# A graph network's attention stage: the pick matrices get 128 rows, and the products that use them read all rows of the turned codes

## The chip, the cores and the metric

The kernel runs on one core of a Trainium2 chip. The metric is the device time of one execution in microseconds (us); lower is better. The core has a matrix engine (TensorE, PE in the profile, with its weight loads as PEld), a vector engine (VectorE, DVE), an activation engine (ScalarE, ACT), GpSimd (POOL), which here issues the indirect transfers, and SyncE (SP), which issues the plain ones. They run on their own and wait for each other through semaphores.

## What is computed

The input is a graph of 6,250 nodes with 64 features and 206,250 edges, sorted by destination. A message network comes first and then two attention layers:

```python
h = relu(layernorm(x))
x = x + L0(h, ...)          # edge MLP, segment sum over row, node MLP
h = relu(layernorm(x))
# attention layer: heads=4, ch=32, then heads=1, ch=64
h = (x @ W).reshape(n, heads, ch)
alpha_src = sum(h * a_src, -1); alpha_dst = sum(h * a_dst, -1)
e = alpha_src[src] + alpha_dst[dst]
e = where(e > 0, e, 0.2 * e)
m = segment_max(e, dst); ex = exp(e - m[dst])
alpha = ex / (segment_sum(ex, dst)[dst] + 1e-16)
out = segment_sum(h[src] * alpha, dst) + b
```

The result is x plus the output of the second layer.

## The kernel before

Nodes lie in 49 tiles of 128. Edges are worked on in groups of 512 (four chunks u of 128), and all edges of a group have their destination in one tile of nodes. There are 452 groups (`GROUPS`) in each attention layer; `LAYERS` gives four heads with 32 channels and then one head with 64.

Every engine runs its own `attend` in a loop over the groups, unrolled by eight (`SLOTS`), and each works on several groups at different stages at once; `of(k)` is the group that entered k steps ago. The order within a step is that of the code, and nothing else. For one group the stages are:

- SP loads the ids of the 512 edges (L521). POOL gathers the table rows of the sources, with four indirect transfers (L690). It waits until the messages of the group eight before are made (`msg_ready`) and its codes are turned.
- DVE turns the lane number of each edge's destination into a code of 16 numbers (`edge_codes`, L1461 to L1477): 0 where a bit agrees and -BIG where it doesn't. ACT makes a matrix of ones and zeros, which says to which lane an edge belongs (`a_hot`, L829 and L836).
- PE transposes that matrix (L1072) and the codes together with the shares of the source (L1076). ACT copies both out of PSUM into `turned` (L853, of which only the first 28 or 19 rows are written, and L855).
- PE multiplies with the pick matrices (L1117), once for each head: the result shows, for each lane and each of 512 edges, the share of the source, or about -BIG where the edge is not the lane's. DVE takes the maximum (`largest_shares`, L1490 for pairs of heads, L1486 for one head), and from it makes the new shift of each node (`new_shifts`, L1516 to L1538).
- PE looks up shares and shifts for each edge (L1088). DVE makes the logits (L1556 to L1567), ACT the exponential (L843), DVE the messages (L1576). ACT makes an f32 copy of `a_hot` (L861).
- PE sums the messages by lane (L1100, f32), and DVE adds them to the node's sum (L1588, L1593).

In a step PE does L1072 and L1076, then L1088, L1100 and last L1117, each for another group. Of the pick products' operands the matrix `picks[n]` has 16 + 3 x heads rows: 28 in layer 0 and 19 in layer 1. It is filled once: cleared on POOL, with ones set by L560, and the first 16 rows copied by DVE. `turned` has 128 rows, eight slots, two halves and 512 columns in bf16; half 0 is the transposed `a_hot`, half 1 the codes.

Ahead of each layer DVE makes the table of node rows (L1422 to L1445) and raises `table_ready`; SP then writes the table to memory (L504), and the gathers start behind that.

Of the kernel before, what the change touches and what calls it, by code (L numbers as in the profile page):

```python
# [13 lines left out]
BF16 = mybir.dt.bfloat16  # L14
# [5 lines left out]
P = 128  # L20
# [27 lines left out]
CODE = 16  # L48
CODE_WORDS = CODE // 2
SLOTS = 8  # L50
# [5 lines left out]
LAYERS = ((HEADS, CH), (1, OUT_DIM))  # L56
# [118 lines left out]
def gnn_kernel(nc, x, ids_in, src_in, dst_next, rec_in, ew1, eb1, ew2, eb2, nw1, nb1, nw2, nb2,  # L175
               W1, a_src1, a_dst1, b1, W2, a_src2, a_dst2, b2, out):
    ctx = ExitStack()
    with ctx:
        def sb(name, shape, dt=F32):
            return ctx.enter_context(nc.sbuf_tensor(name, shape, dt))[tuple(slice(None) for _ in shape)]  # L180

        def sem(name):
            return ctx.enter_context(nc.semaphore(name))
# [32 lines left out]
        spare = sb("spare", [P, SLOTS * U])  # L216
        signs_at = sb("signs_at", [P, NB + 1])

        picks = [sb(f"pick{n}", [CODE + 3 * h, h, P], BF16) for n, (h, _) in enumerate(LAYERS)]
        lower = sb("lower", [P, P])  # L220
        ones = sb("ones", [P, P])
        ones_b = sb("ones_b", [P, P], BF16)
# [53 lines left out]
        def carve(start, shape, dt=F32):  # L276
            words = 1
            for n in shape:
                words *= n
            words = words if dt != BF16 else words // 2  # L280
            v = arena[:, start:start + words]
            assert start + words <= ARENA, (start, shape)
            if dt != F32:
                v = v.bitcast(dt)
            names = " ".join("abcd"[:len(shape)])
            kw = {"abcd"[n]: shape[n] for n in range(len(shape))}
            return v.rearrange(f"p ({names}) -> p {names}", **kw), start + words
# [62 lines left out]
        turned, at = carve(at, [SLOTS, 2, GE], BF16)  # L350
# [21 lines left out]
        def S(name):  # L372
            if name not in s:
                s[name] = sem(name)
            return s[name]
# [3 lines left out]
        class Rounds:  # L379
# [5 lines left out]
            def load(self, i):  # L385
                _, self.values = nc.values_load_multi_w_load_instructions(
                    self.table[0:1, bass.ds(i - self.back, self.count)], engines=(self.engine,), min_val=0, max_val=self.top,
                    skip_runtime_bounds_check_because="counts of comparisons, and starts that a minimum bounds")

            def of(self, g):  # L390
                if g.i is None:
                    return self.eng.value_load(self.table[0:1, bass.ds(g.at, 1)], min_val=0, max_val=self.top)
                return self.values[g.off + self.back]
# [472 lines left out]
        def _(pe):  # L866
# [9 lines left out]
            for k in range(2):  # L876
                pe.matmul(ps[7][:, 128 * k:128 * k + NB], lower, counts[k], start=True, stop=True)
                pe.matmul(ps[7][:, 128 * k + 64:128 * k + 64 + NB], ones, counts[k], start=True, stop=True)
                mm = pe.matmul(ps[7][0:NB, 256 + k:257 + k], counts[k], ones[:, 0:1], start=True, stop=True)
# [3 lines left out]
            for b in range(len(BATCHES) + 1):  # L883
                if b < len(BATCHES):
                    if b > 1:
                        pe.wait_ge(S("own_tt"), b - 1)
                    for u, t in enumerate(BATCHES[b]):
                        mm = pe.transpose(ps[b % 2][0:F_IN, u * P:(u + 1) * P], hs[:, t, :], ident)
                    mm.then_inc(S("own_t"), 1)
                if b > 0:  # L890
# [3 lines left out]
                    for u, t in enumerate(BATCHES[b - 1]):  # L894
                        pe.matmul(ps[2 + (b - 1) % 2][:, u * F_HID:(u + 1) * F_HID], tile_t[0:F_IN, (b - 1) % 2, 0, u * P:(u + 1) * P],
                                  w_dst, start=True, stop=True)
                        mm = pe.matmul(ps[4][:, u * F_HID:(u + 1) * F_HID], tile_t[0:F_IN, (b - 1) % 2, 0, u * P:(u + 1) * P],
                                       w_src, start=True, stop=True)
# [9 lines left out]
            for k in range(3):  # L908
                mm = pe.matmul(ps[4 + k][:, 0:lone], gap_wide[0][0:NT - 1, :], reached[0:NT - 1, k * lone:(k + 1) * lone],
                               start=True, stop=True)  # L910
# [96 lines left out]
            for b in range(len(BATCHES) + 2):  # L1007
                if b < len(BATCHES):
# [4 lines left out]
                    for u, t in enumerate(BATCHES[b]):  # L1013
                        mm = pe.transpose(ps[2 + b % 2][:, u * P:(u + 1) * P], agg[:, t, :], ident)
                    mm.then_inc(S("node_t"), 1)
                if 0 < b <= len(BATCHES):
                    c = b - 1
                    n = len(BATCHES[c]) * P
# [5 lines left out]
                if b > 1:  # L1024
# [4 lines left out]
                    for u, t in enumerate(BATCHES[c]):  # L1029
                        mm = pe.matmul(ps[6 + c % 2][:, u * F_IN:(u + 1) * F_IN], mid_t[:, c % 2, u * P:(u + 1) * P], w_out,  # L1030
                                       start=True, stop=True)
                    mm.then_inc(S("node_out"), 1)

            for n, (heads, ch) in enumerate(LAYERS):
# [5 lines left out]
                for b in range(len(BATCHES) + 1):  # L1040
                    if b < len(BATCHES):
                        if b > 1:
                            pe.wait_ge(S("gat_tt"), before + b - 1)
                        for u, t in enumerate(BATCHES[b]):
                            mm = pe.transpose(ps[b % 2][0:k_in, u * P:(u + 1) * P], node_in[:, t, :], ident)
                        mm.then_inc(S("gat_t"), 1)
                    if b > 0:
# [4 lines left out]
                        for u, t in enumerate(BATCHES[c]):  # L1052
                            mm = pe.matmul(ps[2 + c % 2][:, u * width:(u + 1) * width], tile_t[0:k_in, c % 2, 0, u * P:(u + 1) * P],
                                           gat_w[n], start=True, stop=True)
# [6 lines left out]
                def attend(of):  # L1061


                    g = of(1)
                    if g is not None:
                        r = g.slot(SLOTS)
                        bank = ps[(4, 7)[g.slot(2)]].bitcast(BF16)
                        if g.back(2).exists():
                            pe.wait_ge(S("turned_copied"), g.back(2).done(2))
                        pe.wait_ge(S("a_hot_ready"), g.done())  # L1070
                        for u in range(U):
                            pe.transpose(bank[:, u * P:(u + 1) * P], a_hot[:, r, u, :], ident_b)  # L1072
                        pe.wait_ge(S("code_ready"), g.done(2))
                        pe.wait_ge(S(f"gathered_{r}"), g.uses(SLOTS, 16 * U))
                        for u in range(U):
                            mm = pe.transpose(bank[:, GE + u * P:GE + (u + 1) * P],  # L1076
                                              g_rows[:, r, u * step:u * step + P // 2].bitcast(BF16), ident_b)
                        mm.then_inc(S("turned"), 1)

                    g = of(5)  # L1080
                    if g is not None:
                        pe.wait_ge(S("max_step"), g.done(MAX_STEPS))
                        if g.back(1).exists():
                            pe.wait_ge(S("logit_step"), g.back(1).done(LOGIT_STEPS))
                        lk = look[:, g.slot(4), 0:6 * heads].rearrange("p (k w) -> p k w", k=3)
                        for u in range(U):
                            for part in range(3):
                                mm = pe.matmul(ps[5][:, u * 2 * heads:(u + 1) * 2 * heads], turned[:, g.slot(SLOTS), 0, u * P:(u + 1) * P],  # L1088
                                               lk[:, part, :], start=(part == 0), stop=(part == 2))
                        mm.then_inc(S("looked_up"), 1)  # L1090

                    g = of(7)
                    if g is not None:
                        out_w = width + heads
                        pe.wait_ge(S("a_hot_f_ready"), g.done())
                        pe.wait_ge(S("msg_ready"), g.done())
                        if g.back(1).exists():
                            pe.wait_ge(S("a_added"), g.back(1).done())
                        for u in range(U):
                            mm = pe.matmul(ps[6][:, 0:out_w], a_hot_f[:, g.slot(4), u, :], g_msg[:, g.slot(4), u * out_w:(u + 1) * out_w],  # L1100
                                           start=(u == 0), stop=(u == U - 1))
                        mm.then_inc(S("a_summed"), 1)

                    g = of(2)
                    if g is not None:
                        pe.wait_ge(S("turned_copied"), g.done(2))
                        for h in range(heads):
                            if heads > 1:  # L1110

                                if h % 2 == 0 and g.back(1).exists():
                                    pe.wait_ge(S(f"max_taken{h // 2}"), g.back(1).done())
                            elif g.back(2).exists():
                                pe.wait_ge(S("max_taken0"), g.back(2).done())
                            bank = ps[h] if heads > 1 else ps[g.slot(2)]
                            mm = pe.matmul(bank, picks[n][:, h, :], turned[0:CODE + 3 * heads, g.slot(SLOTS), 1, :], start=True, stop=True)  # L1117
                            if h % 2 == 1 or heads == 1:
                                mm.then_inc(S(f"shown{h // 2}"), 1)

                attention_pipeline(pe, 7, attend, n)

        @block.vector
        def _(dve):
            link = Chain(dve, S("dve_step"))
# [278 lines left out]
            for n, (heads, ch) in enumerate(LAYERS):  # L1404
# [38 lines left out]
                for h in range(heads):  # L1443
                    link(dve.tensor_copy(ac[:, :, h, 0:ch], tb[:, :, at_f + h * ch:at_f + (h + 1) * ch]))
                link(dve.memset(ac[:, :, :, ch:ch + 1], 1.0))  # L1445
                dve.sem_inc(S("table_ready"), 1)

                step = CODE_WORDS + row
# [210 lines left out]
```

## Time and profile before

| | |
|---|---|
| time, median of 3 runs | 9172.81 us (9167.3 to 9173.32) |
| the profiled execution | 9175.25 us, its span 9173.7 us |
| busy: PE | 77% of the span |
| busy: DVE | 66% |
| busy: POOL | 69% |
| busy: ACT | 53% |
| mean granted clock of PE | 0.703 |

The profile page gives the busy time of each engine and, in 40 slices of the span, its share in tenths together with the clock that the chip granted to PE. One slice is 229 us. The edge stage ends at about 4,100 us, layer 0 of the attention runs from 4,320 to 6,745 us and layer 1 from 6,825 to 9,153 us. Other views read the same execution: groups of instructions by line, who waited for whom, the busy time of chosen stretches, the instructions in order of time, and the chain of work that ended last. Instructions of one engine overlap by some tens of nanoseconds, so spacing from start to start is shorter than the durations.

### The profile page before, as it was taken

The numbers are of one execution on the slowest core, as the hardware profiler recorded it, in microseconds if no ns is written. First come the engines' busy times: TensorE is split into PE (matmuls) and PEld (weight loads), VectorE is DVE, ScalarE is ACT, GpSimd is POOL, SyncE is SP. The second block draws the span as 40 slices with busy tenths as digits, with TensorE's granted clock in tenths as the row PEclk, the third lists the DMA queues.
The fourth block names the chain that finished last, engine by engine and source line by source line (L and its number), as shares of the span: only waits on it lengthen the run. The fifth ranks groups of instructions, "written<-read, shape, count | busy, mean of one in ns | idle before, by whom it ended". The sixth has DMA issues, their size and how long they took to land.

```text
span 9173.7 us, 232222 instructions
## 1 busy us (share of the span) xinstructions
PE 7037.3 (77%) x51014; PEld 5502.8 (60%) x51015; DVE 6077.1 (66%) x27239; ACT 4887.5 (53%) x11854; POOL 6338.1 (69%) x7563
## 2 busy tenths in 40 slices
PE   2466666666679999995999999999957777777776
PEld 2355555555568888883566666666635555555554
DVE  7777742222234444444999999999967776676766
ACT  4122233333335455552676767767637777777775
POOL 0377777777777777771777777777737777777775
PEclk9988888888889999996555555555555555555555
DMA  4222222222222222221222222222341111111114
GB/s 141 46 55 55 55 59 60 59 60 60 59 77 80 81 81 80 80 79 25 55 55 54 55 54 54 54 54 55 53 27 28 28 28 28 28 28 28 28 28 27
DMA packets 990523, 491.42 MB, mean 54 GB/s; under 512 B 830665, under 2 KB 841468, under 8 KB 990140
## 3 DMA queue, kind: packets, MB, share of 16 engines
q0 software_dynamic: 168832, 302.29, 15.1%
q1 hardware_dynamic: 701756, 169.41, 10.0%
q10 hardware_dynamic: 119840, 18.68, 1.2%
q8 instruction: 31, 0.51, 0.0%
q14 instruction: 64, 0.52, 0.0%
HBM read 356.46 MB, written 151.48 MB: 55 GB/s over the span
## 4 chain that ended last, share of the span: by engine, by line
PE 24%; issue 24%; POOL 24%; DVE 17%; DMA 6%; DVEq 2%; ACT 1%; POOLq 1%; SPq 0%; ACTq 0%
POOL z_s L640 18%; POOL arena L690 6%; DMA arena<-table,arena 5%; PE ps_all L965 5%; PE ps_all L975 4%; PE ps_all L1100 3%; PE ps_all L992 3%; PE ps_all L989 2%; DVE shift L1531 2%; DVE arena L1535 2%; DVE arena L1490 2%; PE ps_all L1076 1%; DVE arena L1576 1%; PE ps_all L1001 1%; PE ps_all L977 1%
## 5 line engine op out<-in xcount | busy, mean ns | idle before, releaser
L690 POOL DMA_INDIRECT arena<-table,arena x3616 | 3479.3, 962 | 1497.8 <-issue 983.5
L640 POOL DMA_INDIRECT z_s<-arena x1660 | 1758.1, 1059 | 852.4 <-issue 504.2
L1100 PE MATMUL ps_all<-arena 128*128 128x132 f32 (+1 forms) x7232 | 1805.1, 428 | 1.8 <-DVE acc L1593 1.8
L1100 PEld LDWEIGHTS ps_all<-arena 128*128 128x128 f32 x7232 | 1603.0, 324 | 2.6 <-issue 2.6
L829 ACT ACTIVATE arena<-lanes_b,arena 128x128 bf16<-128x128 bf16 x3616 | 1147.3, 387 | 416.7 <-DVE arena L1464 388.5
L1490 DVE TENSOR_REDUCE arena<-ps_all 128x2 f32<-128x1024 f32 x904 | 1096.8, 1213 | 18.3 <-PE ps_all L1117 18.3
L1117 PE MATMUL ps_all<-arena,pick 28*128 28x512 bf16 (+1 forms) x2260 | 1072.1, 591 | 1.8 <-DVE arena L1490 1.8
L1076 PE MATMUL ps_all<-ident_b,arena 128*128 128x128 bf16 x3616 | 537.6, 301 | 651.1 <-DMA arena<-table,arena 445.9
L745 ACT ACTIVATE arena<-ps_all 18x512 f32<-18x512 f32 x415 | 243.6, 587 | 1379.9 <-PE ps_all L952 1376.4
L853 ACT ACTIVATE arena<-ps_all 28x512 bf16<-28x512 bf16 (+1 forms) x904 | 523.4, 579 | 720.1 <-PE ps_all L1076 720.1
L1386 DVE TENSOR_TENSOR arena<-lanes,arena 128x512 f32<-128x512 f32 x452 | 325.4, 720 | 758.4 <-PE ps_all L965 758.4
L950 PE MATMUL ps_all<-ident_b,arena 128*128 128x128 bf16 x1660 | 189.3, 246 | 829.0 <-DVE arena L1334 827.3
L1076 PEld LDWEIGHTS ps_all<-ident_b,arena 128*128 128x128 bf16 x3616 | 353.1, 135 | 768.6 <-DVE arena L1477 403.0
L1341 DVE CAST arena<-arena 128x4 f32<-128x4 int32 x415 | 73.2, 176 | 1042.7 <-DMA z_s<-arena 1042.6
L1072 PEld LDWEIGHTS ps_all<-ident_b,arena 128*128 128x128 bf16 x3616 | 301.8, 127 | 649.4 <-issue 642.7
L950 PEld LDWEIGHTS ps_all<-ident_b,arena 128*128 128x128 bf16 x1660 | 109.6, 107 | 909.0 <-DVE arena L1334 769.5
L1072 PE MATMUL ps_all<-ident_b,arena 128*128 128x128 bf16 x3616 | 533.9, 301 | 102.9 <-ACT arena L836 102.9
L935 PE MATMUL ps_all<-w_edge,arena 128*128 128x128 f32 x3320 | 602.3, 340 | 9.3 <-issue 9.2
L836 ACT ACTIVATE arena<-arena 128x512 bf16<-128x512 bf16 x904 | 568.9, 629 | 30.9 <-ACT arena L829 0.4
L1088 PE MATMUL ps_all<-arena 128*128 128x8 bf16 (+1 forms) x10848 | 446.7, 169 | 179.0 <-DVE arena L1567 173.1
L935 PEld LDWEIGHTS ps_all<-w_edge,arena 128*128 128x128 f32 x3320 | 542.6, 247 | 66.6 <-issue 43.0
L1088 PEld LDWEIGHTS ps_all<-arena 128*128 128x128 bf16 x10848 | 426.7, 108 | 232.9 <-DVE arena L1567 193.0
(260 smaller groups left out, 16049.3 us busy)
## 6 DMA issues: line engine op xcount, KB each, us to landing
arena<-z_s SPq DMA_DIRECT2D x452, 264.0 KB, 2.7
arena<-table,arena POOLq DMA_INDIRECT x3616
arena<-rec_d SPq DMA_DIRECT2D x1660, 10.0 KB
z_s<-arena POOLq DMA_INDIRECT x1660
rec_d<-in_rec ACTq DMA_DIRECT2D x1, 16160.0 KB, 58.2
arena<-ids_d SPq DMA_DIRECT2D x904, 4.0 KB
arena<-pos_d ACTq DMA_DIRECT2D x830, 0.5 KB
arena<-pos_d SPq DMA_DIRECT2D x830, 0.5 KB
```

What stands on the lines that cost most here:

```text
L640: pool.indirect_dma_start(z_s, bass.IndirectOffsetOnAxis(ap=slot[:, g.slot(SLOTS), u:u + 1], axis=0), z_out[:, g.slot(SLOTS), u, :], None) ...
L690: pool.indirect_dma_start(g_rows[:, r, u * step + CODE_WORDS:(u + 1) * step], None, tables[n], bass.IndirectOffsetOnAxis(ap=ids[:, r, 0, u ...
L829: act.activation(lane_gap[:, g.slot(2), u, :], lanes_b, ACT.Square, bias=neg_lane[:, g.slot(4), u:u + 1]).then_inc(S("lane_gap_ready"), 1)
L836: act.activation(a_hot[:, g.slot(SLOTS)], lane_gap[:, g.slot(2)], ACT.Relu, scale=-1.0, bias=1.0).then_inc(S("a_hot_ready"), 1)
L853: act.activation(turned[0:CODE + 3 * heads, g.slot(SLOTS), 1, :], bank[0:CODE + 3 * heads, GE:2 * GE], ACT.Copy).then_inc(S("turned_copied ...
L935: pe.matmul(ps[2 + r][:, u * P:(u + 1) * P], x_t[:, g.slot(4), u * P:(u + 1) * P], w_edge, start=(u == 0), stop=False, skip_group_check=True)
L1072: pe.transpose(bank[:, u * P:(u + 1) * P], a_hot[:, r, u, :], ident_b)
L1076: mm = pe.transpose(bank[:, GE + u * P:GE + (u + 1) * P], g_rows[:, r, u * step:u * step + P // 2].bitcast(BF16), ident_b)
L1088: mm = pe.matmul(ps[5][:, u * 2 * heads:(u + 1) * 2 * heads], turned[:, g.slot(SLOTS), 0, u * P:(u + 1) * P], lk[:, part, :], start=(part ...
L1100: mm = pe.matmul(ps[6][:, 0:out_w], a_hot_f[:, g.slot(4), u, :], g_msg[:, g.slot(4), u * out_w:(u + 1) * out_w], start=(u == 0), stop=(u = ...
L1117: mm = pe.matmul(bank, picks[n][:, h, :], turned[0:CODE + 3 * heads, g.slot(SLOTS), 1, :], start=True, stop=True)
L1490: dve.tensor_reduce(part_max[:, g.slot(4), 2 * pair:2 * pair + 2], ps_all[:, pair * 1024:(pair + 1) * 1024].rearrange("p (h e) -> p h e", ...
```

## The change

The pick matrices get 128 rows, and the rows from 28 (or 19) on stay zero. The product reads all 128 rows of half 1 of `turned`, of which the rows from 28 on have to hold finite numbers; so DVE clears that half once, ahead of layer 0. Everything else stays: the copies into `turned` still write 28 or 19 rows, and the number of matrix products is the same.

```diff
-        picks = [sb(f"pick{n}", [CODE + 3 * h, h, P], BF16) for n, (h, _) in enumerate(LAYERS)]
+        picks = [sb(f"pick{n}", [P, h, P], BF16) for n, (h, _) in enumerate(LAYERS)]
...
-                            mm = pe.matmul(bank, picks[n][:, h, :], turned[0:CODE + 3 * heads, g.slot(SLOTS), 1, :], start=True, stop=True)
+                            mm = pe.matmul(bank, picks[n][:, h, :], turned[:, g.slot(SLOTS), 1, :], start=True, stop=True)
...
                 link(dve.memset(ac[:, :, :, ch:ch + 1], 1.0))
+                if n == 0:
+                    link(dve.memset(turned[:, :, 1, :], 0.0))
                 dve.sem_inc(S("table_ready"), 1)
```

## Rows read from the trace of the kernel before

**Rows 1.** The page: the span, each engine's busy time, and the clock by slice.
```profile
span 9173.7 us, 232222 instructions
...
PE 7037.3 (77%) x51014; PEld 5502.8 (60%) x51015; DVE 6077.1 (66%) x27239; ACT 4887.5 (53%) x11854; POOL 6338.1 (69%) x7563
...
PEclk9988888888889999996555555555555555555555
```

**Rows 2.** Busy time by stretches: PE, PEld, DVE, ACT, POOL, then clock, DMA share, GB/s.
```profile
900.00:2500.00 1600.00, 1011.52 (x7144) 892.80 (x7144) 615.78 (x2651) 495.15 (x894) 1237.45 (x1190) 0.85 0.28 59
2500.00:4100.00 1600.00, 1529.59 (x12641) 1324.92 (x12642) 703.56 (x1440) 764.44 (x1363) 1157.69 (x2298) 0.98 0.29 80
5000.00:6000.00 1000.00, 925.45 (x6081) 612.20 (x6081) 964.66 (x4561) 701.05 (x1901) 731.08 (x759) 0.55 0.26 54
6660.00:6710.00 50.00, 39.07 (x247) 25.59 (x246) 39.19 (x183) 27.58 (x77) 27.94 (x30) 0.50 0.96 43
7000.00:8000.00 1000.00, 746.61 (x5741) 587.80 (x5741) 700.71 (x4554) 709.00 (x1979) 758.85 (x792) 0.50 0.20 28
```

**Rows 3.** Layer 0, 5,000 to 6,000 us: the gathers by line; L1490 by source line.
```profile
L690 POOL DMA_INDIRECT arena<-table,arena x759 | 732.7, 965 | 269.2 <-issue 233.0 <-DVE arena L1576 30.8 <-PE ps_all L1076 5.5
...
L1490 DVE TENSOR_REDUCE arena<-ps_all x381: 1207/1214/1218, 4999.3 to 5999.2; 128x2 f32<-128x1024 f32 x191
```

**Rows 4.** Waits in all of layer 0: us in total, times, longest.
```profile
PE ps_all L1088 <- DVE arena L1567: 171.3, 141, 3.2
DVE arena L1516 <- issue: 75.1, 58, 1.5
POOL arena L690 <- DVE arena L1576: 69.3, 37, 2.2
...
DVE acc L1593 <- PE ps_all L1100: 6.5, 11, 1.3
DVE arena L1490 <- PE ps_all L1117: 5.4, 10, 0.6
```

**Rows 5.** Layer 0, instructions in order of time: start, us, what.
```profile
5501.80 0.16 DVE L1516 TENSOR_SCALAR arena<-dst_parts 128x12 bf16 x1 [1.40 <-issue]
...
5504.42 2.12 PE L1100 MATMUL ps_all<-arena 128*128 128x132 f32 x8
...
5506.47 1.88 PE L1117 MATMUL ps_all<-arena,pick 28*128 28x512 bf16 x4
...
5508.58 0.28 DVE L1593 TENSOR_TENSOR acc<-acc,ps_all 128x132 f32 x1
...
5508.86 1.21 DVE L1490 TENSOR_REDUCE arena<-ps_all 128x2 f32<-128x1024 f32 x1
```

**Rows 6.** Layer 1, 7,000 to 8,000 us: the gathers by line.
```profile
L690 POOL DMA_INDIRECT arena<-table,arena x792 | 759.1, 958 | 241.5 <-issue 185.4 <-DVE arena L1576 56.1
```

**Rows 7.** Layer 0, PE in order of time, in two narrow stretches.
```profile
5505.67 0.87 PE L1100 MATMUL ps_all<-arena 128*128 128x132 f32 x3
...
5507.30 1.05 PE L1117 MATMUL ps_all<-arena,pick 28*128 28x512 bf16 x2
5508.29 0.29 PE L1072 MATMUL ps_all<-ident_b,arena 128*128 128x128 bf16 x1
```

**Rows 8.** The chain that ended last, where layer 0 drains: start, us, what.
```profile
6735.11 1.98 PE ps_all L1100 x8
```

**Rows 9.** Waits in the last groups of layer 0, 6,600 to 6,760 us.
```profile
DVE arena L1490 <- PE ps_all L1117: 4.9, 9, 0.6
```

**Rows 10.** A long memset by line; the table's way out and the first gather.
```profile
L1359 DVE MEMSET arena<- 128x4224 f32 x1 | 3.6, 3578 | 1.1 <-issue 1.1
...
4299.07 0.40 SPq L504 DMA_DIRECT2D table<-tab  x1
...
4319.02 1.00 POOL L690 DMA_INDIRECT arena<-table,arena  x1 [180.74 <-DMA arena<-ids_d]
```

**Rows 11.** POOL at the start, in order of time.
```profile
5.80 3.45 POOL L560 TENSOR_SCALAR_AFFINE_SELECT pick<-pick 28x512 bf16<-28x512 bf16 x6
```

## The prediction, made before the change was run

> **What bounds the kernel now.** I read the page first [rows 1], then the busy time by stretches [rows 2], because the change touches one stage only. The two attention layers fill the second half of the span, some 4,320 to 9,155 us. There the granted clock of TensorE (PE) lies at 0.50 to 0.55, which is its lower level, 1.2 GHz; in the edge stage before, it was 0.98, near the upper level of 2.4 GHz. In layer 0 both PE (925 of 1,000 us) and VectorE (DVE, 965) look full, so the share of busy time does not say which one sets the pace. In layer 1 nobody is above 76%.
>
> What ended the waits does say it. In layer 0 [rows 3], GpSimd (POOL) issued 759 gathers in 1,000 us, 190 groups, so a group takes 5.27 us. Over the whole layer [rows 4] DVE waited for PE only 6.5 + 5.4 us in some 2,400, while PE waited 171 us for DVE, and POOL 69 us for DVE's message product (L1576). The one regular hole in DVE is 75 us before L1516, 58 times some 1.4 us, put down to "issue": DVE's own queue loading registers at the head of each round of eight groups (one of them, 1.40 us, stands in [rows 5]). So DVE is packed and sets the pace, PE follows it, and POOL follows too: its own cost is 0.965 us for a gather [rows 3] and 0.30 us between two, 4 x 1.265 = 5.06 us for a group. In layer 1 [rows 6] it is POOL alone: 792 gathers in 1,000 us, 958 ns each and the same gap, 4 x 1.263 = 5.05 us, which is the period (1,000 / 198 = 5.05).
>
> How far PE is from mattering in layer 0 is read from one group [rows 5]. PE's sums (L1100) end at 5,506.54 and DVE takes them (L1593) at 5,508.58, 2.0 us later. The four pick products (L1117) end at 5,508.35; DVE starts on the first pair at 5,508.86, at which time even the second pair is done. Every result of PE that DVE reads in that group has been lying ready.
>
> **The change part by part.**
> *Row counts of the pick products.* In layer 0 there are 4 x 452 of them, in layer 1 452. Each still streams 512 columns. At the lower clock their spacing is 0.42 us [rows 7]: two take 1.05 us together, and the last alone some 0.63; 512 columns at 1.2 GHz are 0.43 us, so the rows do not enter, and I leave the product itself at its price.
> *The change of shape.* Between the last 128-row sum and the first 28-row product lies a gap. The sums are spaced (0.87 - 0.43) / 2 = 0.22 us, the last of them starts at 6.11 us, a next one would start at 6.33, and the first pick product starts at 6.47 [rows 5, 7]: 0.14 us late. Behind the pick products the same: the last starts at 7.72, the next instruction is due at 8.15 and starts at 8.29, again 0.14. If the gap comes of the row counts, the change gives PE 0.28 us for each group, 0.28 x 904 = 253 us of PE time over both layers. Bounds: 0 (the gap is the wait for the bank or the copied codes) and 253 us; I take 253, since neither wait shows as a releaser of PE in [rows 4]. None of it is on the path while DVE (layer 0) or POOL (layer 1) sets the pace. The Trainium skill (TensorEngine Tiling (Array Packing), Key Properties) says that a change of tiling mode drains the engine. The trace agrees with a lag of 0.14 us each way; were PE the bound, the rule would be worth all of those 253 us.
> *The clock.* The stretch 900 to 2,500 us had PE busy 63% of the time at clock 0.85; layer 0 has 93% at 0.55 [rows 2]. Layer 0 is where a part of the products uses 28 rows. So the full-row products may lift the clock there, at most to the upper level, where PE's work would take some half of its time. Layer 1 has one pick product for each group and a lot of idle time; I expect 0.50 to stay. The Trainium skill (TensorE: Matmul & The Clock Gate, Part 1: The HAM clock gate) has the clock follow how busy PE has been; the trace differs, since the busier stretch has the lower clock. By the rule as it stands the change would move nothing, as the busy share stays what it was.
> *What a faster PE is worth.* The upper bound is what DVE waited for PE in layer 0, 12 us [rows 4], and PE's pieces on the chain where a layer drains: four sums of 1.98 us or so (one of them in [rows 8]) and a few short products, about 9 us in each layer, half of it at the upper clock, 4.5 x 2 = 9. Together 21 us. The lower bound is 0. In the last groups of each layer the gathers themselves are the limit: the DMA engines are 96% busy (6,660 to 6,710 us in [rows 2]), and PE waits for them; nothing is to be had there. Of the 5.4 us that DVE waits for L1117, 4.9 lie in those last groups [rows 9]. I take 2 us: the ten waits for L1117 lose 0.14 us each, and the clock stays low in the drain, where PE is idle longest.
> *The new memset.* It clears 8 x 512 bf16 for each partition on DVE, just before the semaphore that starts the table's way out, so it delays everything by its length: the first gather starts 20 us later behind the table's way out and the loads of the ids [rows 10]. A memset of 4,224 f32 took 3.58 us, 0.85 ns an element: 4,096 elements are 3.5 us. If bf16 goes at a quarter of that it is 0.9 us. I take 3.5; no row shows bf16 faster.
> *The picks.* POOL's memset and selects on them act on 128 rows rather than 28 and 19, with the same length in each row. They run in the first 10 us [rows 11], long before DVE needs them. Zero; if each took twice as long it would be some 4 us, still hidden behind DVE's normalisation.
>
> *Sum*, on the profiled execution's own 9,175.25 us (span 9,173.7): +3.5 - 2 = +1.5, 9,176.75. That execution lies 2.4 us above the median of the runs, 9,172.81, so the median after should be 9,174.3, say 9,174. Nothing else is late next: DVE in layer 0 and POOL in layer 1 have no instruction fewer.
>
> **The rivals.**
> *The clock rises and every wait on PE goes.* For it: the clock row. Against it: the waits are mostly behind gathers. 9,172.8 + 3.5 - 21 = 9,155. That is 0.19% below, on the line between same and faster.
> *PE is the hidden pacemaker of layer 0.* DVE would be packed only because it trails PE. Then with a faster PE the layer runs at POOL's pace, 5.27 to 5.05 us for a group, 0.22 x 452 = 99 us: 9,172.8 + 3.5 - 99 = 9,077. Against it: the 171 us that PE waits for DVE and the 2 us that results lie ready. It decides if DVE's waits, not its own work, make up the 5.27 us.
> *Slower: 128 rows read beside a packed DVE.* During L1117 (1.7 us of each group) PE would now read 100 more partitions, in the memory where DVE works. DVE is packed, so every delay passes to the end. If its work beside L1117 took 3% longer, that is 0.05 us for each group, 452 x 0.05 = 23 us, with the memset 9,199. It decides from 0.03 us for a group on (15 us with the 3.5 make 0.2%). Against it: L1490 takes 1,207 to 1,218 ns in 381 cases [rows 3], whatever PE reads beside it, and part of them lie beside products of 128 rows.
> *Nothing changes on PE*: the gaps stay and the clock too. 9,172.8 + 3.5 = 9,176.
>
> **How the numbers follow.** Forecast 0.78 (9,165 to 9,181); the clock and all waits 0.08, half of it same and half faster; hidden pacemaker 0.05; slower 0.05; nothing on PE 0.04, same. Faster by over 0.2%: 0.04 + 0.05 = 0.09. Slower: 0.05. Same: 0.86. (0.2% is 18 us, about what a measurement of this kernel can tell from no change.) The range goes from the clock case, 9,155, to the top of the forecast with the memset at twice its price, 9,182.
>
> **What would show it.** The gaps before L1117 and L1072 should go, spacing 0.22 and 0.43 us right through. PE's busy share in layer 0 falls, its wait for DVE grows by 0.28 us a group or more. The granted clock of 5,000 to 6,000 us rises above 0.55 or doesn't; either way DVE stays at 965 of 1,000 us and POOL at 759 gathers. A new row L1447 or so shows the memset. I am wrong if DVE's idle time or the length of its instructions changes in layer 0, or if the gathers of layer 1 come closer together than 1.26 us.

## The result, and the profile after

| | before | after |
|---|---|---|
| time, median | 9173.06 us (9167.3 to 9176.62) | 9379.54 us (9377.34 to 9382.25) |
| ratio, with its 95% interval | | 1.0228 (1.0215 to 1.024) |
| span of the profiled execution | 9173.7 us | 9379.4 us |

The change costs 206 us. The forecast was 9,174 us in a range of 9,155 to 9,182, so it was wrong, by far more than the range allowed.

The page of the changed kernel, with the same lines as [rows 1] and the one line of its DMA queues that moved:

```profile
span 9379.4 us, 232223 instructions
...
PE 6460.7 (69%) x51014; PEld 5272.9 (56%) x51015; DVE 6092.3 (65%) x27240; ACT 4887.5 (52%) x11854; POOL 6342.9 (68%) x7563
...
PEclk9988888888889999996787777777865555555555
...
q14 instruction: 329, 2.70, 0.1%
```

There is one instruction more on DVE, whose busy time was 6,077.1 us before; PE has 577 us less work, since in layer 0 its clock stands at 7 to 8 tenths rather than 5. DVE and POOL work 15 and 5 us longer, and the span is 205.7 us longer all the same. The last line is the queue that brings instructions to the engines: 329 packets and 2.70 MB, where the kernel before had this:

```profile
q14 instruction: 64, 0.52, 0.0%
```

Both counts give 8.2 KB for a packet (the trace's records say 8,192 B). There are 265 packets more, which is 5 x 53.

Where the time lies is read from the first and the last gather (L690) of each layer, here by source line: count, shortest, median and longest ns, then first and last start. Before, layer 0:

```profile
L690 POOL DMA_INDIRECT arena<-table,arena x1808: 951/958/1463, 4319.0 to 6705.4; - x181
```

and layer 1:

```profile
L690 POOL DMA_INDIRECT arena<-table,arena x1808: 952/958/1013, 6824.4 to 9114.4; - x181
```

After, layer 0 and layer 1:

```profile
L690 POOL DMA_INDIRECT arena<-table,arena x1808: 950/956/1469, 4317.9 to 6910.3; - x181
...
L690 POOL DMA_INDIRECT arena<-table,arena x1808: 949/956/1203, 7033.9 to 9320.5; - x181
```

The layer 0 stretch grows from 2,386.4 to 2,592.4 us, +206.0. The start is 1.1 us earlier, the pause between the layers 4.6 longer (123.6 against 119.0), layer 1 is 3.4 shorter and the tail 0.4: together 205.7. All of the loss is in layer 0.

The stretches of [rows 2] after the change (busy PE, PEld, DVE, ACT, POOL, clock, DMA share, GB/s):

```profile
5000.00:6000.00 1000.00, 657.37 (x5556) 456.76 (x5557) 885.23 (x4171) 641.91 (x1739) 674.15 (x694) 0.79 0.24 51
7500.00:8500.00 1000.00, 704.99 (x5761) 600.46 (x5759) 706.28 (x4560) 710.39 (x1982) 758.47 (x794) 0.50 0.20 28
```

In layer 0 POOL issued 694 gathers instead of 759, and DVE, which had been packed, is idle for 115 us in 1,000 instead of 35. The waits of layer 0, as in [rows 4], say where:

```profile
PE ps_all L1088 <- DVE arena L1569: 752.0, 402, 10.3
...
POOL arena L690 <- DVE arena L1578: 278.6, 59, 9.1
DVE arena L1518 <- issue: 278.4, 60, 8.6
```

PE and POOL wait for DVE, and DVE waits for nobody: L1518 (it was L1516; the new lines move what follows by two) is the head of a round of eight groups. What was 75.1 us in 58 holes, 1.5 at the longest, is 278.4 in 60: 203 us more, nearly the whole loss. One such head in the chain that ended last, first before (start, us, what; DVEq is DVE's own queue, L118 the loop's branch, L386 the loading of registers):

```profile
5499.98 0.06 DVEq L118
5500.03 0.18 DVE arena L1538
5500.22 0.09 DVE arena L1475
5500.31 0.04 DVE arena L1477
5500.35 0.04 issue
5500.40 1.10 DVEq L386
```

then after:

```profile
5503.82 0.09 DVE arena L1477
5503.91 0.08 DVE arena L1479
5503.99 3.57 issue
5507.56 0.09 DVEq L118
5507.68 1.10 DVEq L386
```

Before, the branch takes 0.06 us and the loading of 16 registers begins 0.4 us behind it, while DVE works off L1538 to L1477. After, nothing comes out of DVE's queue for 3.57 us; nothing in the profile holds it, which is what "issue" means. By the trace's records the branch itself began at 5,503.93, and the L118 at 5,507.56 is the first instruction of the next turn, so the hole stands between a branch and its target. The loading takes the same 1.10 us. In order of time L1518 then shows the whole hole, 5.10 us, where [rows 5] has 1.40:

```profile
5509.09 0.16 DVE L1518 TENSOR_SCALAR arena<-dst_parts 128x12 bf16 x1 [5.10 <-issue]
```

Round by round (from one branch of the loop to the next, from the trace's records): a median of 42.18 us before and 46.08 after. 3.9 x 53 turns that go back to the loop's head = 207 us, the loss.

The loop of layer 0 is 358 instructions long by their places in DVE's program (357 in the expectations below is the distance from the first to the last); the records with a source line are 356 for a turn. If a packet of 8,192 B holds 128 instructions of 64 bytes, the loop is 358 x 64 = 22.9 KB long: it fits into three packets if it lies well, and else touches four. The 128 are an assumption at this point, which the shifts below bear out. That gave the theory.

### The profile page after: what moved, and what is told of

The parts are those of the page before. It is cut to its first block, busy times and chain, and to the rows that moved or that the text cites. A ratio compares the mean times of both kernels' runs of the same rounds, so it can differ in the third digit from the quotient of the medians.

```text
span 9379.4 us, 232223 instructions
## 1 busy us (share of the span) xinstructions
PE 6460.7 (69%) x51014; PEld 5272.9 (56%) x51015; DVE 6092.3 (65%) x27240; ACT 4887.5 (52%) x11854; POOL 6342.9 (68%) x7563
## 4 chain that ended last, share of the span: by engine, by line
issue 27%; POOL 22%; PE 19%; DVE 16%; ACT 6%; DMA 5%; DVEq 2%; POOLq 1%; ACTq 0%; SPq 0%
POOL z_s L640 18%; DMA arena<-table,arena 5%; POOL arena L690 5%; PE ps_all L965 5%; PE ps_all L975 4%; PE ps_all L992 3%; ACT arena L829 3%; PE ps_all L989 2%; DVE arena L1492 2%; PE ps_all L1076 1%; ACT arena L861 1%; DVE shift L1533 1%; DVE arena L1537 1%; DVE arena L1578 1%; PE ps_all L1001 1%
## 5 line engine op out<-in xcount | busy, mean ns | idle before, releaser
L690 POOL DMA_INDIRECT arena<-table,arena x3616 | 3489.2, 965 | 1697.2 <-issue 967.9
L1100 PE MATMUL ps_all<-arena 128*128 128x132 f32 (+1 forms) x7232 | 1597.5, 390 | 1.8 <-DVE acc L1595 1.8
L1100 PEld LDWEIGHTS ps_all<-arena 128*128 128x128 f32 x7232 | 1419.3, 290 | 2.5 <-issue 2.5
L1492 DVE TENSOR_REDUCE arena<-ps_all 128x2 f32<-128x1024 f32 x904 | 1097.0, 1214 | 14.9 <-PE ps_all L1117 14.9
L1117 PE MATMUL ps_all<-arena,pick 128*128 128x512 bf16 x2260 | 949.9, 513 | 83.5 <-DVE arena L1492 83.0
L1076 PE MATMUL ps_all<-ident_b,arena 128*128 128x128 bf16 x3616 | 461.5, 269 | 782.5 <-DMA arena<-table,arena 510.0
L1076 PEld LDWEIGHTS ps_all<-ident_b,arena 128*128 128x128 bf16 x3616 | 281.7, 117 | 935.3 <-DVE arena L1479 511.9
L950 PE MATMUL ps_all<-ident_b,arena 128*128 128x128 bf16 x1660 | 188.7, 245 | 814.8 <-DVE arena L1334 814.7
L861 ACT ACTIVATE arena<-arena 128x512 f32<-128x512 bf16 x904 | 553.3, 612 | 0.0
```

Source lines behind the costliest of these rows:

```text
L690: pool.indirect_dma_start(g_rows[:, r, u * step + CODE_WORDS:(u + 1) * step], None, tables[n], bass.IndirectOffsetOnAxis(ap=ids[:, r, 0, u ...
L861: act.activation(a_hot_f[:, g.slot(4)], a_hot[:, g.slot(SLOTS)], ACT.Copy).then_inc(S("a_hot_f_ready"), 1)
L1076: mm = pe.transpose(bank[:, GE + u * P:GE + (u + 1) * P], g_rows[:, r, u * step:u * step + P // 2].bitcast(BF16), ident_b)
L1117: mm = pe.matmul(bank, picks[n][:, h, :], turned[:, g.slot(SLOTS), 1, :], start=True, stop=True)
L1492: dve.tensor_reduce(part_max[:, g.slot(4), 2 * pair:2 * pair + 2], ps_all[:, pair * 1024:(pair + 1) * 1024].rearrange("p (h e) -> p h e", ...
```

## The experiments

**The theory, F (fetch):** one more DVE instruction ahead of layer 0's loop moves the loop so that it reaches into a fourth block of 128 instructions. With three blocks a turn finds its code in the engine's store, with four it has to be fetched again at every turn, and DVE stands still. **The rivals:** R, products of 128 rows slow DVE or the gathers, or the new clock does; M, the memset of `turned` itself does it, by its size or by what it touches; P, any DVE instruction more costs it, wherever the loop lies. (The recorded expectations call F theory A, R theory B, M theory C and P theory E; their D is a single bad place.) The runs fell into three groups, on two chips that differ a little (the kernel before took 9,139.94, 9,166.86 and 9,142.92 us on them), so each is compared with the runs of before beside it.

### The memset alone, on the kernel before

```diff
                 link(dve.memset(ac[:, :, :, ch:ch + 1], 1.0))
+                if n == 0:
+                    link(dve.memset(turned[:, :, 1, :], 0.0))
```

> The kernel before with the memset alone; products still read 28 and 19 rows. Theory A, fetch: the one more instruction on DVE ahead of layer 0 moves its loop so that a round no longer fits what the engine holds of its program, and each of 54 rounds refetches: 9,379 us, a gap of some 3.6 us behind the loop's branch, some 330 packets on the instruction queue of the trace rather than 64. Theory B, rows and clock: the loss comes of the faster PE or of the rows read, so this kernel takes 9,173 + 3.5 = 9,176 us and the packets stay at 64.

Measured: 9,364.33 us against 9,139.94, ratio 1.0248 (1.023 to 1.0265), 329 instruction packets, a round of 45.97 us. The picks have 28 rows here and the clock stays where it was:

```profile
5000.00:6000.00 1000.00, 862.45 (x5601) 572.38 (x5600) 886.53 (x4194) 645.78 (x1750) 679.26 (x699) 0.54 0.23 51
```

The memset brings 224 us by itself, without the rows and without the clock. In this group of runs the two kernels below that keep the loop's place have rounds of 41.53 and 41.63 us, so the round is some 4.4 us longer here.

### The rows alone: the clearing moved from DVE to POOL

```diff
+            pool.wait_ge(S("mlp_done"), 1)
+            pool.memset(turned[:, :, 1, :], 0.0).then_inc(S("turned_clear"), 1)
+            pool.wait_ge(S("turned_clear"), 1)
...
-                if n == 0:
-                    link(dve.memset(turned[:, :, 1, :], 0.0))
```

> The changed kernel with the clearing moved from DVE to POOL, which is idle there; DVE's program is instruction for instruction that of before. Theory A: no refetching, 64 packets, DVE's round in layer 0 back at 42.2 us, 9,167 to 9,175 us, while the clock of layer 0 stays at 0.79 as in the changed kernel. Theory B: the loss stays, 9,376 us.

Measured: 9,143.5 us against 9,139.94, ratio 1.0004 (0.9995 to 1.0014), 64 packets, a round of 41.53 us. The same stretch, with 128-row products:

```profile
5000.00:6000.00 1000.00, 697.99 (x6060) 476.05 (x6154) 963.82 (x4630) 710.50 (x1927) 761.22 (x772) 0.85 0.25 55
```

DVE is packed again (963.8 of 1,000) and the gathers are as close as ever. The maximum that reads PSUM while PE now reads 100 partitions more keeps its length (1,207/1,214/1,218 ns before, [rows 3]); after the change, in its own stretch:

```profile
L1492 DVE TENSOR_REDUCE arena<-ps_all x348: 1207/1214/1219, 5004.3 to 5998.9; 128x2 f32<-128x1024 f32 x174
```

So R falls: rows and clock together are worth nothing that can be measured, in either direction.

### A tiny memset in the same place

```diff
                 link(dve.memset(ac[:, :, :, ch:ch + 1], 1.0))
+                if n == 0:
+                    link(dve.memset(zero, 0.0))
```

> The kernel before with one more memset of a single column (60 ns) at the same place on DVE, nothing else. Theory A: the place counts and not the work: 9,376 us, the same 3.6 us gap. Theory C, the memset itself (its 4 KB in each partition, its tile): 9,173 us. Theory B: 9,173 us.

Measured: 9,362.97 us, ratio 1.0246 (1.0229 to 1.0263), 329 packets, a round of 45.82 us. It touches nothing that the loop uses, and it took 59 ns. M falls.

### The change with one other instruction less

```diff
-                link(dve.memset(tb[:, :, 0:at_s], 0.0))
+                if n == 1:
+                    link(dve.memset(tb[:, :, 0:at_s], 0.0))
```

This leaves the clearing of a part of layer 0's table out, so that the program ahead of the loop is as long as it was; all of the change is in.

> The changed kernel with one other DVE instruction ahead of layer 0 taken out (the memset L1430 of the part columns, which in layer 0 the copies behind it fill completely), so that the loop lies where it lay before. Theory A: 9,173 us plus 2, rounds of 42.2 us, 64 packets. Theory B or C: 9,379 us.

Measured: 9,143.64 us, ratio 1.0002 (0.9992 to 1.0011), 64 packets, a round of 41.63 us. The change, with its big memset on DVE, costs nothing that can be measured if the count of instructions stays. (The memset left out took 0.30 us in the kernel before, so it is not its work that came back.) What remains is P against F: both say that one more is dear. They part where many more are added.

### Shifts of 64, 120 and 160

On the kernel before, with 64, 120 or 160 in the place of N:

```diff
+                if n == 0:
+                    for _ in range(N):
+                        link(dve.memset(zero, 0.0))
```

> The kernel before with 64 tiny memsets ahead of layer 0's loop on DVE, each waiting for the one before: 64 x 0.12 = 8 us by the row of the 16 memsets at the start. Theory A, the place of the loop body (357 instructions) against blocks of the engine's instruction store: still in the bad range, so before + 8 + 210. If it were chance or a single bad place (theory D): before + 8.

> 120 tiny memsets, 14 us. A body of 357 or so instructions lies within three blocks of 128, or two of 256, once the shift is over some 100: before + 14, no refetching. If every shift is bad because the program as a whole grew (theory E): before + 14 + 210.

> 160 tiny memsets, 19 us. With blocks of 128 instructions (8 KB, the size of the packets) the body lies across four again: before + 19 + 210. With blocks of 256 it still lies within two: before + 19; then layer 1's loop lies across three and refetches, some 3.6 us in each of 54 rounds, which DVE's idle time in layer 1 (30%) should hide: no more than 10 us on top.

| shift | time, before 9,166.86 | ratio | packets | round |
|---|---|---|---|---|
| 64 | 9,368.49 | 1.022 (1.0202 to 1.0239) | 595 | 45.48 us |
| 120 | 9,181.16 | 1.0016 (1.0006 to 1.0026) | 65 | 42.12 us |
| 160 | 9,347.11 | 1.0197 (1.0178 to 1.0215) | 595 | 45.17 us |

120 added instructions cost 14.3 us, which is 0.12 us each: their own length and no more. 64 cost 202 us. P falls, a single bad place (D) falls with the 64, and a fetch is what goes by place. 160, which is 128 and 32 more, is dear again, though less so: 180 us, of which some 19 are the memsets' own length. That is what a period of 128 instructions gives. In the kernel before, the loop must end right at the end of a block: a loop of 358 in three blocks of 128 leaves room for 26, and yet a shift by one is too much. From there a shift of 1 to 101 or so should be dear and one of 102 to 128 cheap. With blocks of 256, a loop that ended at a border would lie well for shifts from about 102 to 256, and 160 would have been cheap.

With 64 and 160 there are 595 packets, 266 more than 329. These shifts move layer 1's loop as well (352 instructions to its branch), and it is fetched again too.

### On either side of the border: shifts of 98 and 104

The same edit with 98 and 104, one execution of each.

> 98 tiny memsets ahead of layer 0's loop, 12 us. Theory A with blocks of 128 instructions: before the change the body (357 instructions) ends in the last slot of a block and starts 357 slots before, so it lies in three blocks up to a shift of 0, in four from 1 to 100 or 101, in three again from 101 or 102. So here still four: before + 12 + 205, and 64 + 265 instruction packets or 64 + 530 (if layer 1's body straddles too).

> 104 tiny memsets, 12.5 us. Six instructions more than in the run with 98, and by theory A the body lies in three blocks again: before + 12.5, some 65 packets. A slow slide of the time with the shift, or a loss that goes with the program's length, would give before + 200 here as well.

Measured, with before at 9,142.92: 9,348.65 us, 595 packets and a round of 45.23 us at 98; 9,165.54 us, 65 packets and 41.77 us at 104. The border lies between them, where blocks of 128 put it. It also measures the block: if the loop ends with a block at a shift of 0, the first cheap shift is 358 less two blocks, so a block has between (358 - 104) / 2 = 127 and (358 - 99) / 2 = 129.5 instructions, and 8,192 B over 128 are 64 B for each. These are single executions, but they are 183 us apart. At 104 the time is 22.6 us above before, 10 more than the memsets' own 12.5; a single execution does not say why.

### The instruction at the very start

```diff
+            link(dve.memset(zero, 0.0))
```

It doubles the first instruction that the kernel gives to DVE, some 1,800 ahead of the loop.

> One tiny memset more as DVE's very first instruction, where it waits for the input anyway: every loop of DVE moves by one slot. Theory A: before + 205, 329 packets, as if the instruction stood right ahead of the loop. If what stands next to the loop matters: before + 0.

Measured: 9,366.06 us, ratio 1.024 (1.0211 to 1.027), 329 packets, a round of 46.02 us. In time it is over 4 ms ahead of the loop. Only the count matters.

### The same fetch in layer 1

64 tiny memsets again, but ahead of layer 1's loop alone (`if n == 1`).

> 64 tiny memsets ahead of layer 1's loop alone, 8 us. By theory A layer 0 stays as it was and layer 1's body lies across four blocks: 64 + 265 packets, a stall at each of its 54 rounds. DVE has 30% of its time free there and POOL sets the pace, so none of it reaches the end: before + 8. If a stall of DVE's queue is lost wherever it falls: before + 8 + 190.

Measured: 9,153.81 us against 9,142.92, ratio 1.0011 (0.9999 to 1.0022), 330 packets: 266 more than before, in layer 1 now. The hole is there (DVE's waits, 7,000 to 9,000 us):

```profile
DVE arena L1519 <- issue: 205.5, 50, 4.4
```

But a round stays at 40.39 us (40.44 before), and in that stretch POOL waits no longer for DVE than it did. The first line is before, the second this run:

```profile
POOL arena L690 <- DVE arena L1576: 111.9, 367, 0.3
```

```profile
POOL arena L690 <- DVE arena L1579: 84.4, 277, 0.3
```

The 10.9 us are some 8 of added instructions and a rest near the bound of the measurement. DVE is busy 700 of 1,000 us in layer 1, so four microseconds in a round of 40 are absorbed; in layer 0 DVE is the pacemaker, and they reach the end. From the branch to the next instruction of DVE's queue it is 2.87 us here (median) and 2.81 in layer 0 with the 64 ahead of it: a fetch of the same size has two prices.

### A shorter round head

If DVE's queue at the head of a round is on the path, then the 1.40 us that the kernel before spends there must be worth something too. It loads 16 numbers into registers, of which 12 are used.

```diff
-                buckets = Rounds(dve, mybir.EngineType.DVE, bucket_of, NT - 1, SLOTS, 2 * SLOTS)
+                buckets = Rounds(dve, mybir.EngineType.DVE, bucket_of, NT - 1, SLOTS, SLOTS + 4)
```

> The kernel before with DVE loading 12 registers at the head of a round rather than 16 (the four not loaded are read by nobody); the program keeps its length. If the head's stall in layer 0 is DVE time on the path, as read before the change: 1.10 us x 4/16 = 0.28 us less in each of 54 rounds, 15 us faster, ratio 0.9984. If another wait takes its place (POOL, the ring of eight slots): no change.

Measured: 9,153.11 us against 9,166.86, ratio 0.9985 (0.9976 to 0.9994), 64 packets, a round of 41.80 us. The loading by itself, in the chain:

```profile
5026.68 0.85 DVEq L386
```

1.10 has become 0.85 us, 0.063 a register. 0.25 x 54 = 13.5 us, and 13.8 were measured (the interval reaches from 6 to 22): what DVE's queue spends at the head of a round in layer 0 comes out at the end, one to one as far as this can tell. This version is a little faster than the kernel before.

## Why the prediction was wrong

**The step that failed** is the memset in the part on the change, and with it the sentence that nothing else is late next. I costed an added instruction by its duration alone: "+3.5". Its duration was even less than that:

```profile
L1447 DVE MEMSET arena<- 128x2048 uint32 x1 | 1.8, 1765 | 0.5 <-DVE acc L1445 0.5
```

The 4,096 bf16 ran as 2,048 uint32, and it took 1.77 us, 0.86 ns for each uint32: the price of an element in [rows 10] was right, the count of elements half of the one I took. What cost 206 us was that it is one instruction more, ahead of a loop that, as the cheap and the dear shifts say, filled its blocks to the last place. None of the rivals had this. The slower one, 9,199, was another mechanism and a ninth of the size.

**What could have been seen.** The rows of before had both halves of it. [Rows 4] and [rows 5] showed that the queue of DVE, not only its work, stands on the path at each head of a round. I read 1.4 us there as a fixed cost and asked what nobody had to pay for. The page of before had 64 packets on the queue of instructions, too few for a loop that is fetched again at every turn (53 x 5 are 265); how near the loop was to that, no row says, and only its place in the program would have shown it. What the prediction should have carried is a rival with a price: if the loop no longer fits, a fetch for each round, on the engine that sets the pace. Its price had no row.

The Trainium skill (Runtime: NRT & Kernel Launch, Instruction fetch mechanics) names the mechanism: the engine's store is refilled in blocks, and a taken branch whose target is not among the blocks that are held has to wait for a fetch. The runs agree that this happens: from the branch to the next instruction of DVE's queue it is 0.29 us before and 3.68 after (medians of layer 0). They differ in the sizes. The page has blocks of 16 KiB and holds two of them; here the packets are 8,192 B, the pattern has a period of 128 instructions, and a loop over three such blocks is not fetched again while one over four is.

**What bounds the kernel: right.** DVE sets the pace in layer 0. The loss itself shows it, since a hole in DVE's queue went to the end whole, and so, within its interval, does the shorter round head. The hidden pacemaker (9,077) falls: without the place's cost, PE's clock went up to 0.85 and its work in 1,000 us down from 925 to 698, and the ratio was 1.0004.

**The gap between shapes: right, a little too large.** In layer 1 the clock is 0.50 in both kernels, so PE's busy time can be compared: 746.6 us in 1,000 before [rows 2] (the same 746.6 from 7,500 to 8,500) and 704.99 after, with some 198 groups in either. That is 0.21 us for each group, where I took 0.28. The gaps themselves stand in the records of that stretch, as medians from start to start: from the last sum to the pick product 350 ns before and 213 after, from there to the next transpose 534 and 427. So they lost 0.14 and 0.11 us, 0.24 together, where I took 0.14 twice. The kernel with the memset alone keeps 350 and 534, and the change with one instruction less has 213 and 427: the gaps came of the row counts and not of a wait. Each product by itself is no shorter; in layer 1, 7,500 to 8,500 us, before:

```profile
L1117 PE MATMUL ps_all<-arena,pick 19*128 19x512 bf16 x198 | 119.2, 602 | 0.0
...
L1076 PE MATMUL ps_all<-ident_b,arena 128*128 128x128 bf16 x792 | 117.5, 303 | 253.4 <-DMA arena<-table,arena 163.5 <-DVE arena L1477 87.5 <-DVE arena L1475 2.3
```

and after:

```profile
L1117 PE MATMUL ps_all<-arena,pick 128*128 128x512 bf16 x198 | 124.9, 631 | 0.0
...
L1076 PE MATMUL ps_all<-ident_b,arena 128*128 128x128 bf16 x795 | 118.0, 303 | 295.0 <-DMA arena<-table,arena 183.6 <-DVE arena L1479 108.7 <-DVE arena L1477 2.7
```

The idle time ahead of L1076 grew by 41.6 us, from 253.4 to 295.0, which is what PE's work lost: PE got time and spent it waiting. That it was off the path was right as well.

**The clock: open before, and now seen.** I left it open for layer 0 and expected 0.50 to stay in layer 1. It rose from 0.55 to 0.79 (0.85 without the hole) in layer 0, and stayed in layer 1. Of its worth, which I put between 0 and 21 us, the upper end is excluded: both versions that carry the rows and keep the loop's place are within 4 us of before, and their intervals reach from 0.9992 (7 us faster) to 1.0014. The 2 us that I took cannot be told from nothing.

**The picks on POOL and the first gather: right.** The first gather started at 4,317.9 us, before at 4,319.0.

**The chances.** 0.86 on no change that can be measured came from adding up durations on the right engine. Without the shift that forecast would have held (9,143.5 and 9,143.64 against 9,139.94). I had written that I would be wrong if DVE's idle time changed in layer 0, and that is what changed.

## What stays open

The fetch is shown by the packets and the period; how many blocks the store holds beyond three was not measured, and neither was which of the five packets of a turn DVE waits for. The hole is not of one size. From the branch to the next instruction of DVE's queue the median is 3.68 to 3.81 us in the four kernels with layer 0's loop shifted by 1, and two of the five packets begin in between; it is 2.81 to 2.85 at shifts of 64, 98 and 160, and one packet begins in between. Where three blocks suffice it is 0.29. The rounds go with it only roughly: they are 3.9 to 4.4 us longer at a shift of 1, and 3.1 (160) to 3.6 (98) at the others, each against kernels of its own group of runs that are not fetched again. What of a packet's place makes the difference was not tried. Why the clock rises with full rows in layer 0 and not in layer 1 was not tried either. That the last instruction of the loop sits at the end of a block in the kernel before is inferred from which shifts are dear, not read from an address.

## What to carry to other kernels

An instruction added ahead of a loop costs its length and also moves the loop: on the engine that sets the pace, look at the packets of the instruction queue before and after, since 265 more of them went with the whole loss here. A loop of some hundreds of instructions that is fetched again at every turn is worth shortening or moving by a few instructions, and where a measured difference comes with an edit that could hardly make it, run the edit's neutral twin (the same count of instructions, none of the work) before any theory about the work. The head of a round on the packed engine is on the path, the loading of registers too.

## What the runs showed of the hardware

- DVE's program comes in packets of 8,192 B; the shifts of 98 and 104 put 127 to 129 instructions in one. A loop of 358 instructions ran without being fetched again when it lay in three of them, and with five packets for each turn when it lay over four (265 for 53 turns). Cheap shifts were 0, 104 and 120, dear ones 1, 64, 98 and 160.
- The fetch made the wait behind the branch 2.8 to 3.8 us instead of 0.29 and the round of layer 0 longer by 3.1 to 4.4 us; in layer 1, on an engine busy 70% of the time, the round was no longer (40.39 against 40.44 us).
- Loading 16 registers took 1.10 us and 12 took 0.85.
- In layer 1, pick products of 128 rows instead of 19 shortened the steps beside them, start to start: 350 to 213 ns ahead of the pick product and 534 to 427 behind it, at the 1.2 GHz level.
- With all 128 rows in every product, TensorE's granted clock in layer 0 was 0.79 and 0.85 as a mean of the stretch, between 1.2 GHz (0.5) and 2.4 GHz (1.0), with PE busy 657 and 698 of 1,000 us. With the 28-row products among them it was 0.55 at 925 busy. Clock and busy share did not go together here.
- A DVE memset of 4,096 bf16 for each partition ran as 2,048 uint32, in 1.77 us.
